# A factorization machine: three tiles of x fetched in whole rows, small loads moved to GpSimd's queue, constant products on TensorE

## The reference

```
xf = x.astype(V.dtype)
xv = xf @ V                                   # 512 x 64
sum_sq = jnp.sum(xv * xv, axis=-1)
sq_sum = xf @ jnp.sum(V * V, axis=-1)
y = g_bias + xf @ bias + (0.5 * (sum_sq - sq_sum))[:, None]
```

## Time and profile before

| | |
|---|---|
| device time, three runs | 47.59, 47.24, 46.98 us; median 47.24 us |
| profiled execution: device time | 46.84 us |
| its span | 44.7 us |
| TensorE, VectorE busy | 21.5 us, 24.3 us |
| ScalarE, GpSimd busy | 32.2 us, 27.2 us |
| read from HBM | 14.48 MB |

### The profile page before, as it was taken

One profiled execution on the slowest core, in us unless ns is written; L12 is line 12 of the kernel. 1 busy time (PEld: TensorE's weight loads), 2 busy tenths in 40 slices (PEclk: granted clock), 3 DMA queues, 4 the chain that ended last, 5 costly groups with the idle time before them and its releaser, 6 DMA issues.

```text
span 44.7 us, 659 instructions
## 1 busy us (share of the span) xinstructions
PE 21.5 (48%) x208; PEld 19.8 (44%) x208; DVE 24.3 (54%) x74; ACT 32.2 (72%) x34; POOL 27.2 (61%) x50
## 2 busy tenths in 40 slices
PE   0000000000400000019999999999978956999700
PEld 0000000000400000019999989998948936989500
DVE  2100976029929899999900772170049129399930
ACT  0007999429962999599999899993039999999400
POOL 1899999999999999999999998100000020000000
PEclk9999999999999999999999999999999999999997
DMA  0299999999999999999999999999999999820000
GB/s 0 57 335 171 165 210 226 247 232 141 118 106 105 103 104 105 103 102 105 103 103 103 104 104 103 103 105 114 101 105 102 100 99 102 59 15 0 0 0 2
DMA packets 6540, 4.87 MB, mean 109 GB/s; under 512 B 1647, under 2 KB 5770, under 8 KB 6538
## 3 DMA queue, kind: packets, MB, share of 16 engines
q0 software_dynamic: 5184, 3.21, 82.6%
q1 hardware_dynamic: 874, 0.85, 7.1%
q10 hardware_dynamic: 480, 0.79, 5.4%
HBM read 14.48 MB, written 0.00 MB: 324 GB/s over the span
## 4 chain that ended last, share of the span: by engine, by line
POOL 43%; DMA 28%; ACT 19%; issue 2%; DVE 2%; POOLq 0%; ACTq 0%
DMA x_all<-in_r_x_dram 28%; POOL x_all L181 28%; ACT v_sq L303 19%; POOL wall L243 15%; DVE xv L384 1%; DVE xv_sq L389 1%; POOL odd_cast L248 1%; DVE foreign L446 0%; POOLq L243 0%; DVE general L452 0%; DVE foreign_any L448 0%; ACTq L301 0%; POOLq L531 0%; DVE y_sb L389 0%
## 5 line engine op out<-in xcount | busy, mean ns | idle before, releaser
L495 PE MATMUL xv_ps<-wall,x_all 128*128 128x195 bf16 x192 | 19.4, 262 | 8.9 <-DVE x_all L376 8.9
L495 PEld LDWEIGHTS xv_ps<-wall,x_all 128*128 128x128 fp8e4 x192 | 17.7, 104 | 9.7 <-issue 7.6
L303 ACT ACTIVATE v_sq<-x_all,minus_half 128x6272 bf16<-128x6272 fp8e4 (+1 forms) x4 | 19.5, 4881 | 2.7 <-DMA x_all<-in_r_x_dram 2.5
L181 POOL DMA_DIRECT2D x_all<-in_r_x_dram x36 | 19.5, 548 | 0.9 <-POOLq L531 0.9
L376 DVE STREAM_TRANSPOSE x_all<-x_all 128x384 uint32<-128x384 uint32 (+2 forms) x18 | 8.4, 507 | 10.1 <-DMA x_all<-in_r_x_dram 10.1
L339 DVE TENSOR_TENSOR v_rest<-v_in 128x512 f32<-128x512 f32 (+1 forms) x6 | 4.0, 704 | 5.7 <-DMA v_in<-in_L_rec_V_dram 5.6
L243 POOL TENSOR_TENSOR wall<-v_rest 128x512 bf16<-128x512 f32 (+1 forms) x6 | 6.6, 1118 | 0.1
L248 POOL CAST odd_cast<-x_all 128x128 bf16<-128x128 fp8e4 x4 | 1.2, 302 | 8.6 <-DMA x_all<-in_r_x_dram 8.6
L484 PE MATMUL g_ps<-g_in,ones 1*128 1x1 f32 x2 | 0.6, 344 | 11.8 <-DMA g_in<-in_L_rec_g_bias_dram 11.8
L484 PEld LDWEIGHTS g_ps<-g_in,ones 1*128 1x128 f32 x2 | 0.5, 308 | 11.8 <-issue 11.8
L281 ACT ACTIVATE v_sq<-v_in 128x512 f32<-128x512 f32 (+1 forms) x6 | 3.8, 632 | 1.5 <-DMA v_in<-in_L_rec_V_dram 1.5
(11 more groups left out here) (30 smaller groups left out, 9.1 us busy)
## 6 DMA issues: line engine op xcount, KB each, us to landing
x_all<-in_r_x_dram POOLq DMA_DIRECT2D x16, 100.0 KB, 11.5
x_all<-in_r_x_dram POOLq DMA_DIRECT2D x12, 96.0 KB, 10.8
v_in<-in_L_rec_V_dram ACTq DMA_DIRECT2D x6, 128.0 KB, 6.3
v_in<-in_L_rec_V_dram SPq DMA_DIRECT2D x6, 128.0 KB, 5.3
x_all<-in_r_x_dram POOLq DMA_DIRECT2D x4, 64.0 KB, 12.8
x_all<-in_r_x_dram POOLq DMA_DIRECT2D x4, 32.0 KB, 12.5
v_in<-in_L_rec_V_dram SPq DMA_DIRECT2D x4, 8.0 KB, 5.2
bias_in<-in_L_rec_bias_dram SPq DMA_DIRECT2D x3, 7.0 KB
```

The source lines that it names most:

```text
L181: queue.dma_start(x_words[S * i:S * i + S, t, :, lo // QUAD:hi // QUAD].bitcast(fp8), rows[:, :, START[i] + lo:START[i] + hi]).then_inc(x_ ...
L303: nc.scalar.activation(squares[:, :, 0:S + d1 * W], words.bitcast(fp8), ACT.Square, bias=minus_half[:, 0:1], accum_out=from_half[:, n:n + ...
L495: last = nc.tensor.matmul(xv_ps[t][:, :, :], rows[:, q, :], wall[:, QUAD * d + q, :, 0:E], start=(d + q == 0), stop=(u == LAST_TURN[T - 1] ...
```

## The change

- Tiles 0, 1 and 2 of x are one piece each (1568 columns of a quarter in one run); tile 3 keeps its three pieces. 24 DMAs for x in place of 36.
- On GpSimd's queue now stand, between the two halves (by quarters) of tile 0: bias, the odd rows, the last third of V and g. SyncE and ScalarE issue the first two thirds of V only.
- g is added at each tile's start, by a product of ones with a row that is zero but for g (L483 of the new kernel); the product behind each tile goes.
- TensorE runs 16 float32 products of `ones` with itself (L486) once four middle parts are placed, ahead of the first tile.
- The first piece of tile 3 is turned in four steps in place of two (`cuts`): TensorE's first share of it is smaller.
- ScalarE checks the last 256 columns of tile 3 too; VectorE drops L440, L446 and L448 and reduces the bits of the 512 columns in between. TensorE sums bits and squares in one accumulator by six products at its end, and VectorE compares that with one number.

```diff
-    PIECES = [(t, d, d + 6) for t in range(T - 1) for d in (0, 6)] + [(T - 1, 0, 6), (T - 1, 6, 10), (T - 1, 10, ND)]
-    FIRST_PIECE = [2 * t for t in range(T)]
+    PIECES = [(t, 0, ND) for t in range(T - 1)] + [(T - 1, 0, 6), (T - 1, 6, 10), (T - 1, 10, ND)]
+    FIRST_PIECE = list(range(T))
     TURNS = []
     for k, (t, d0, d1) in enumerate(PIECES):
-        for s in range(d0 // PAIR, d1 // PAIR, 3):
-            end = min(s + 3, d1 // PAIR)
+        cuts = [0, 1, 3] if (t, d0) == (T - 1, 0) else list(range(d0 // PAIR, d1 // PAIR, 3)) + [d1 // PAIR]
+        for s, end in zip(cuts, cuts[1:]):
             TURNS += [(k, t, s, end, [h]) for h in range(PAIR)]
     LAST_TURN = [max(u for u, turn in enumerate(TURNS) if turn[1] == t) for t in range(T)]
-    ODD_BEHIND = LAST_TURN[:T - 1] + [LAST_TURN[T - 2] + 2]
+    ODD_BEHIND = LAST_TURN[:T - 1] + [LAST_TURN[T - 2] + 4]
     V_LOADS = [(0, 4), (4, 8), (8, 12)]
-    HALVES = [(t, ND) for t in range(T - 1)] + [(T - 1, 6)]
+    CHECKS = [(t, 0, ND, [t]) for t in range(T - 1)] + [(T - 1, 0, 6, [T - 1]), (T - 1, 10, ND, [T + 1])]
+    CHECKED = sum(W * (d1 - d0) + (S if d0 == 0 else 0) for _, d0, d1, _ in CHECKS)
+    WARM_UP = 16
...
-        g_in = sb("g_in", [1, 1], fp32)
+        g_in = sb("g_in", [1, PARTS, E], fp32)
...
+        def load_odd(queue):
+            for i in range(NQ):
+                queue.dma_start(v_in[S * i:S * i + S, NC - 1, :], V[START[i]:START[i] + S, :]).then_inc(odd_landed, 16)
+
+        def load_bias(queue):
...
+
+        def load_x(queue, k, quarters=range(NQ)):
             t, d0, d1 = PIECES[k]
             lo, hi = (S + d0 * W if d0 else 0), S + d1 * W
             rows = x.rearrange("(g r m) l -> m r g l", r=S, m=T)[t]
-            for i in range(NQ):
+            for i in quarters:
...
-            for n in range(NL):
+            for n in range(NL - 1):
...
-            sp.wait_ge(bias_cleared, 1)
...
-            sp.dma_start(g_in[:, :], g_bias.rearrange("(a b) -> a b", b=1)).then_inc(g_landed, 16)
-            for i in range(NQ):
-                sp.dma_start(v_in[S * i:S * i + S, NC - 1, :], V[START[i]:START[i] + S, :]).then_inc(v_landed[NL - 1], 16)
...
-            load_x(pool, 0)
-            load_x(pool, 1)
-            load_x(pool, 2)
+            load_x(pool, 0, (0, 1))
+            pool.wait_ge(bias_cleared, 1)
+            load_bias(pool)
+            load_odd(pool)
+            load_v(pool, NL - 1, range(NQ))
+            pool.wait_ge(g_cleared, 1)
+            pool.dma_start(g_in[:, 0, F:E], g_bias.rearrange("(a b) -> a b", b=1)).then_inc(g_landed, 16)
+            load_x(pool, 0, (2, 3))
             place_low(0)
             place_low(1)
-            load_x(pool, 3)
+            load_x(pool, 1)
             place_low(2)
             place_low(3)
-            load_x(pool, 4)
+            load_x(pool, 2)
             place_low(4)
             place_low(5)
             cast_odd(0)
+            load_x(pool, 3)
+            cast_odd(1)
+            load_x(pool, 4)
             load_x(pool, 5)
-            cast_odd(1)
-            load_x(pool, 6)
-            load_x(pool, 7)
-            load_x(pool, 8)
             cast_odd(2)
             cast_odd(3)
...
         def _(act):
-            for n in range(NL):
+            for n in range(NL - 1):
                 load_v(act, n, (2, 3))
...
-            for n, (t, d1) in enumerate(HALVES):
-                nc.vector.memset(quarters[:, n:n + 1], 0.25 * GT * (S + d1 * W)).then_inc(quarters_set, 1)
+            nc.vector.memset(g_in[:, :, :], 0.0).then_inc(g_cleared, 1)
...
-            dve.wait_ge(v_landed[NL - 1], V_COUNT[NL - 1])
+            dve.wait_ge(odd_landed, 16 * NQ)
...
-            turn(first)
-            turn(first + 1)
+            for u in range(first, first + 4):
+                turn(u)
             turn_odd(T - 1)
             combine(T - 2)
-            turn(first + 2)
-            turn(first + 3)
+            turn(first + 4)
+            turn(first + 5)
...
-            turn(first + 4)
-            turn(first + 5)
+            turn(first + 6)
+            turn(first + 7)
             dve.wait_ge(masked, 1)
-            nc.vector.scalar_tensor_tensor(groups, part_words(T - 1, 5, 6), TOP_BITS, groups, ALU.bitwise_and, ALU.bitwise_or
-                                           ).then_inc(x_seen, 1)
-            dve.wait_ge(x_seen, 2)
-            nc.vector.tensor_reduce(foreign[:, 4:5], seen[:, :], AX.X, ALU.max).then_inc(foreign_found, 1)
-            dve.wait_ge(half_squared, len(HALVES))
-            dve.wait_ge(quarters_set, len(HALVES))
-            nc.vector.tensor_tensor(foreign[:, 0:4], from_half[:, :], quarters[:, :], ALU.not_equal).then_inc(foreign_found, 1)
-            dve.wait_ge(foreign_found, 2)
-            nc.vector.tensor_reduce(foreign_any[:, :], foreign[:, :], AX.X, ALU.add).then_inc(foreign_ready, 1)
+            nc.vector.tensor_reduce(seen_any[:, :], seen[:, :], AX.X, ALU.max).then_inc(seen_ready, 1)
             combine(T - 1)
 
             dve.wait_ge(foreign_summed, 1)
-            nc.vector.tensor_scalar(general[0:1, 0:1], foreign_ps[0:1, 0:1], 0.0, None, ALU.is_gt).then_inc(general_ready, 1)
+            nc.vector.tensor_scalar(general[0:1, 0:1], foreign_ps[0:1, 0:1], 0.25 * P * GT * CHECKED, None, ALU.not_equal
+                                    ).then_inc(general_ready, 1)
...
-            nc.tensor.matmul(g_ps[:, 0:1], ones[0:1, :], g_in[0:1, 0:1], start=True, stop=True).then_inc(g_spread, 1)
+            nc.tensor.matmul(g_ps[:, 0:1], ones[0:1, :], g_in[0:1, 0, F:E], start=True, stop=True).then_inc(g_spread, 1)
+            for t in range(T):
+                nc.tensor.matmul(xv_ps[t][:, :, :], ones[0:1, :], g_in[0:1, :, :], start=True, stop=False)
+            pe.wait_ge(mid_placed, 4)
+            for _ in range(WARM_UP):
+                nc.tensor.matmul(gen_ps[:, 0:P], ones[:, :], ones[:, :], start=True, stop=True)
...
-                                                start=(d + q == 0), stop=(u == LAST_TURN[T - 1] and d == ND - 1 and q == QUAD - 1))
+                                                start=False, stop=(u == LAST_TURN[T - 1] and d == ND - 1 and q == QUAD - 1))
                 if u == ODD_BEHIND[t]:
                     pe.wait_ge(odd_turned_ready, t + 1)
-                    nc.tensor.matmul(xv_ps[t][:, :, :], odd_turned[:, t, :, :].rearrange("p g r -> p (g r)"),
-                                     wall[:, NC - 1, :, 0:E], start=False, stop=False)
-                    last = nc.tensor.matmul(xv_ps[t][:, 0, F:E], ones[0:1, :], g_in[0:1, 0:1], start=False, stop=(t < T - 1))
+                    last = nc.tensor.matmul(xv_ps[t][:, :, :], odd_turned[:, t, :, :].rearrange("p g r -> p (g r)"),
+                                     wall[:, NC - 1, :, 0:E], start=False, stop=(t < T - 1))
                 if u == LAST_TURN[t]:
                     last.then_inc(multiplied, 1)
-            pe.wait_ge(foreign_ready, 1)
-            nc.tensor.matmul(foreign_ps[0:1, 0:1], foreign_any[:, :], ones[:, 0:1], start=True, stop=True
-                             ).then_inc(foreign_summed, 1)
+            pe.wait_ge(seen_ready, 1)
+            nc.tensor.matmul(foreign_ps[0:1, 0:1], seen_any[:, :], ones[:, 0:1], start=True, stop=False)
+            for n in range(len(CHECKS)):
+                pe.wait_ge(half_squared, n + 1)
+                last = nc.tensor.matmul(foreign_ps[0:1, 0:1], from_half[:, n:n + 1], ones[:, 0:1], start=False,
+                                        stop=(n == len(CHECKS) - 1))
+            last.then_inc(foreign_summed, 1)
```

More of the change, by code:

```diff
@@ L124, in factorization_machine @@
         v_landed = [sem(f"v_landed{n}") for n in range(NL)]
+        odd_landed = sem("odd_landed")
         bias_landed = sem("bias_landed")
@@ L129, in factorization_machine @@
         bias_cut = sem("bias_cut")
[L130 to L131 removed]
+        g_cleared = sem("g_cleared")
         consts_set = sem("consts_set")
@@ L151, in factorization_machine @@
         y_ready = sem("y_ready")
-        foreign_ready = sem("foreign_ready")
+        seen_ready = sem("seen_ready")
         half_squared = sem("half_squared")
@@ L164, in factorization_machine @@
         g_added = sem("g_added")
-        V_COUNT = [16 * (NQ + (NQ if n == NL - 1 else 0)) for n in range(NL)]
+        V_COUNT = 16 * NQ
         def load_v(queue, n, quarters):
@@ L174, in load_v @@
                 ).then_inc(v_landed[n], 16)
-        def load_x(queue, k):
+        def load_odd(queue):
+            for i in range(NQ):
+                queue.dma_start(v_in[S * i:S * i + S, NC - 1, :], V[START[i]:START[i] + S, :]).then_inc(odd_landed, 16)
+        def load_bias(queue):
+            queue.dma_start(bias_in[0:1, W2 - S:W2], bias[0:S, :].rearrange("l o -> o l")).then_inc(bias_landed, 16)
+            queue.dma_start(bias_in[1:1 + NS, :], bias[S:Q, :].rearrange("(s l) o -> s (l o)", l=W2)
+                            ).then_inc(bias_landed, 16)
+            for i in range(1, NQ):
```

(18 more changed lines are left out.)

8 lines of the change are left out of this document (3 added, 5 removed).

## The result

Device time of the change: 47.95, 48.05, 49.77 and 47.97 us, median 48.01; before, with one run more, median 47.11. The ratio is 1.022 (95% interval 1.012 to 1.031), about 2% slower. The run of 49.77 us is left out of the ratio; its mean granted clock was 0.964 where the other three had 1.0, and it has no trace. The profiled execution took 47.95 us with a span of 45.9 us, 1.2 us over before's 44.7.

The account below looks back on a forecast made before the run. The stream of x, ScalarE and TensorE were taken to bound the kernel closely together. TensorE's end -0.2, its clock +1.7 and the flag +0.1 gave +1.6 us on 46.84: 48.4 us, range 46.2 to 49.6.

Parts of the forecast that it names:

- the term that made up nearly all of the forecast: TensorE starts tile 2 at 1.2 GHz after an idle gap: +1.67 us, bounds 0 and 4.2.
- my first rival: TensorE's clock stays up, or falls between tiles 0 and 1 instead: 46.4 to 47.3 us, chance 0.25.
- The bound now: Before the change, three things lie close together: the stream of x, ScalarE's checks, and TensorE, whose last product ends at 42.10 us.
- Transfers of x: Whole rows of x speed the stream by 0.65 us by the end of tile 2, bounds nothing and 1.3 us.
- The price of a run: Each run in x's DMAs costs 6.8 ns; a whole row replaces two runs and saves one, 0.22 us a tile.
- The landing at 32.4: Tile 2 of x lands at 32.4 us, 0.65 earlier than the 33.05 before.
- my third rival: GpSimd's queue starves the stream of x: later landings slide by 1 to 2 us, 49.4 to 50 with the clock, chance 0.1.
- GpSimd's queue: 14 small DMAs at 0.25 to 0.55 us each; first low part at 9 us (7.1 to 11.3); cost 0.
- Tile 0 can so start some 2 us earlier.: On TensorE, since V's second third shares its engines less and bias moves up; worth 0 at the end.
- the gap in which the clock was to fall: TensorE idle for 3.6 us before tile 2, from 29.5 to 33.05 us, where before there was 0.5.
- The clock: TensorE's clock falls in an idle gap of 3.6 us, so tile 2 starts at 1.2 GHz: 1.67 us.
- The end: TensorE runs tiles 2 and 3 without a wait, to 43.6 us; ScalarE, done at 42.7, is covered; flag adds 0.1.

Follow-up runs that it names:

- e6: The kernel before with the change's flag, g and turns of tile 3; loads and halves of x as before, no constant products: ratio 0.985 to before.
- e7: e6 with ScalarE checking tile 2 in its two halves: ratio 0.991 to before over ten runs.
- e2: The change, but GpSimd's first two low parts wait until VectorE has made its fourth rest: ratio 1.055 to before.
- e3: The change without ScalarE's check of tile 3's last 256 columns; VectorE looks at their bits as before: ratio 1.022 to before.
- e4: The change without the 16 constant products: ratio 1.032 to before.
- e1: The change with bias, g, odd rows and V's last third back on SyncE's and ScalarE's queues: ratio 1.017 to before.
- e5: The kernel before with one edit, tiles 0, 1 and 2 of x in whole rows: ratio 1.028 to before.
- e8: e1 with tile 0 of x in two halves as before, tiles 1 and 2 in whole rows: median 47.41 us beside 47.05 for before.
- e9: e8 with 12 more constant products behind tile 1, in the wait for tile 2: median 47.10 us beside 47.01 for before.
- e10: e7 with tile 1 of x alone in whole rows: ratio 1.004 to before.

## Why the prediction was right in size and wrong in its steps

That the time came out inside the range is luck: the term that made up nearly all of the forecast was absent, and terms that I had put at nothing took its place. The case in which the clock stays up was my first rival (0.25), but its 46.4 to 47.3 us missed the measured 47.95 too.

- **The bound now.** Right in that ScalarE and TensorE end together; the wider error was to take one profile's landing of tile 2 (33.07) as the kernel's. With the same transfers it was 31.63 and 31.38 in e6 and e7.
- **Transfers of x.** The price of a run was right: from 22 to 30 us the stream went at 105 to 107 GB/s in the traces with whole rows and no halves in flight, and at 103 in before, e6 and e7. The landing at 32.4 failed: 33.43, outside the bounds. The traces with the small loads on GpSimd's queue have 33.43, 33.45 and 33.32 (the change, e2, e3), and 35.1 in e4; whole rows with those loads on the other queues have 32.24 and 31.95 (e1, e5). So the move goes with a landing about 1.3 us later. By single traces that is weak, as landings with the same transfers differ by up to 1.7 us; but the rate from 14 to 20 us parts the kernels without exception: 97, 96, 89 and 80 GB/s in the change, e2, e3 and e4, and 103 to 109 in the eight others. This is the starving of my third rival, to which I gave 0.1. That the late issue of tile 1 (13.3 us) is its cause is argued; no run changes that alone.
- **GpSimd's queue.** The 14 small DMAs took 0.50 to 0.56 us each, my upper bound from its own row. The first low part began at 10.84; I took 9, and priced the delay at nothing.
- **"Tile 0 can so start some 2 us earlier."** The step that failed: tile 0 began 4.6 us later than before (24.52 against 19.94), and with it went the gap in which the clock was to fall. I had counted what V gains from less traffic on its own queues, and not two other things. The first is what other queues lose to longer runs on GpSimd's. The Trainium skill ("DMA: Bandwidth & Descriptors", Queues, rings and completion order) says that an engine takes turns between its queues packet by packet. e5 and e8 agree with that rule: weights 3.4 us later with long runs beside V, and back at 19.2 with short ones. The second is what the late low parts do to VectorE, and in the change itself this is the larger part: e3 and e4 have V on time and late weights. A low part beside a subtraction holds it up. The Trainium skill ("SBUF — State Buffer", Who interferes with whom) says that a VectorE instruction with two SBUF inputs and a GpSimd instruction that reads SBUF exclude each other. The 3.09 against 1.29 us of e2 agree. The constant products then held tile 0 for another 1.5 us; e4 shows that this cost nothing, as without them tile 0 ran slowly and tile 1 ended at 33.3 as well.
- **The clock.** The mechanism was right. e8 shows it: 3.14 us without work, granted clock 0.50, 5.61 us for a tile in place of 4.35 (1.3 us, I had 1.67). e9, with the gap filled and no such fall in four runs, agrees. In the change it had only 0.85 us to act in, as weights and constant products were late. The term was 0 in the three runs with a mean clock of 1.0.
- **The end.** The last two tiles took 34.06 to 42.75, 8.69 us (I had 8.88). ScalarE was said to be covered by a slow TensorE. With the clock up it wasn't: its fifth check ended 1.16 us after the last product. I had the 1.34 us right and priced it at nothing.
- So +1.6 forecast and +1.1 in the profiled execution: the clock's 1.7 was missing, and ScalarE's check, later weights and a later landing stood in its place.

## What to carry to other kernels

Here the length of the runs in one queue changed what the other queues got (e5, e8): lengthen rows where nothing urgent is in flight beside them, not at the start. Work that is put on an engine's queue delays what stands behind it there, and what that then runs beside can cost more than the delay (e2, e3). When a wait is merged (one semaphore for a whole tile), ask how long the multiplying engine stands idle before it and what that does to its clock; lateness elsewhere can hide the answer. An operation that is added to an engine is free only while the engine said to cover it is the slower one in every case of the forecast.

## What was not expected of the hardware

- The clock can fall in some runs of a kernel and not in others: e8 had 47.04 to 47.81 us with a mean granted clock of 0.963 or less, and 46.07 with 1.0. How much of this is the clock's is open, since e9 had 46.08 to 47.30 with 0.992 or more. An idle gap of 2.44 us (e4) and of 3.14 us (e8) before tile 2 was followed by the lower level; one of 1.98 us before tile 2 (e3) and one of 1.33 before tile 3 (e10) weren't.
- With the same transfers tile 2 landed at 31.38 to 33.07 us (before, e6, e7), and at 33.32 to 35.11 (the change, e3, e4). That is more than most of what is tuned here; one trace doesn't price a wait.
- A VectorE operation of 16 columns took 1.74 us (e2, from 15.90 us, with a low part from 16.55), and 0.18 us before.
- GpSimd needs as long to issue a DMA of one element (0.53 us for g) as one of 128 runs (0.54 us).
